# A decoder layer on one core: the cross-attention sums and gates in TensorE column groups, the normalisations on ScalarE, and another order on every engine

## The chip, the core and the metric

The kernel runs on one core of a Trainium2 chip. The metric is the device time of one execution in microseconds, the median of several runs.
Engines: PE is TensorE (PEld its weight loads), DVE is VectorE, ACT is ScalarE, POOL is GpSimd, SP is SyncE, which here only issues DMAs.

## The reference, cut to what matters

The input is 64 sequences of 128 tokens with 512 features; each goes through three steps, each followed by a residual and a layer normalisation.

```
x = layernorm(x + attn(x));  x = layernorm(x + xattn(x, ctx, ctx));  x = layernorm(x + ffn(x))

attn:   q, k, v = x @ W.T + b (rotary on q, k); per token, its 16 heads of 32 attend to each other; @ Wo.T + bo
xattn:  q = x, k = v = ctx, 16 heads of dh = 32, causal
        ig, fg   = concat(q, k, v) @ Wi + bi,  ... @ Wf + bf          # (token, head)
        log_D    = cumsum(log_sigmoid(fg)) differences + ig, masked to s >= t
        D        = exp(log_D - max_log_D);  C = (q k^T / sqrt(dh)) * D
        Cn       = C / (max(|C.sum(-1)|, exp(-max_log_D)) + 1e-6)
        h        = Cn @ v;  each head of h normalised over its 32 features, * ln_scale
ffn:    eight experts score each token; the best one applies a rank-8 update and a bias
```

## The kernel before

One sequence is one tile of 128 tokens by 512 features, and the tiles go through a software pipeline. In step a, each engine works on tile a and on older ones: b = a-1, c = a-2, d = a-3 and so on. The order of the pieces inside a step is written out by hand, once for each engine; a piece waits on semaphores of the pieces that it reads from. There are 64 tiles and 6 steps more to drain (`LAGS`).

The pieces, by their names in the code: `p_*` makes q, k, v of tile a or b; `a_S`, `a_O`, `a_proj` are the attention among heads; `m_*` is the cross-attention; `r_*` its head normalisation and residual; `x_*` the experts and the output.
q, k, v and the projection are `product` (L365 to L368; v is L355 to L360): twelve matmuls of 512 columns each. The other matmuls are float32, and each stands as two instructions in the trace.

What the change touches, tile by tile:

- `m_gate` (L460, L462): the gates of tile c, from x1T and cT, in eight matmuls with 48 stationary columns, summed in one place.
- `m_gs`, `m_abs`, `m_softplus`, `m_scan`: log-sigmoid, running sum `Fs`, `a_row`, running maximum `M_row` and `FM`, on 16 partitions, shared between ACT and DVE.
- `spread_M` (SP): `M_row` goes out to DRAM and comes back broadcast over the partitions into `Mb` (1 MB). `m_Dx` (ACT, L642) makes 16 exponentials of 128x128 from it, `m_mask` (POOL, L739) cuts them to the triangle, `m_QK` (PE, L481) makes the products of q and k in four row groups, and `m_C` (DVE, L913) multiplies the two into `Dx`.
- `m_c1` (PE, L448): the context times a centring matrix, so that every head has mean zero; ACT copies it to `c1`, which has a 33rd column of ones for each head.
- `heads` (PE, L493): 16 matmuls, each with a 128x128 block of `Dx` as the stationary operand and 33 columns of `c1` moving; ACT copies the result to `Hs` (`m_Hs`, L650).
- `r_norm`, `r_var`, `r_pow` (POOL, L746), `r_y` (DVE, L939), `r_y2` and `r_r2` (POOL): head normalisation and residual.
- three layer normalisations: statistics on DVE (`norm_stats`), `rsqrt` by a power on POOL (L760), and then `a_x1` (L884), `r_x2` (L952), `x_yo` (L1021), each a subtract and multiply over 512 columns, on DVE.

In PE's step the end of one step and the start of the next read:

```
m_QK(c)  m_x1T(b)  x_F(e)  x_LT(f) | m_gate(c)  a_S(b)  m_H(d)  heads(d, 0, 5)  p_v(b)  heads(d, 5, H)  p_v_rest(b)
m_cT(b)  m_aT(c)  m_c1(c)  p_VG(b)  x_Y(g)  p_xT(a)  a_O(b)  x_x2T(e)  p_q(a)  a_proj(b)  p_k(a)
```

Of the kernel before, what the change touches and what calls it, by code (L numbers as in the profile page):

```python
# [20 lines left out]
ALU = mybir.AluOpType  # L21
# [31 lines left out]
LAGS = 6  # L53
PADS = 7
# [48 lines left out]
def bass_decoder(nc, x, ctx, wq, wk, wv, wo, bqkv, bo, rope, ident, mask_l, mask_r, head_rows,  # L103
                 w_gate, b_gate, ln_scale, w_expert, debias, degen, expert_rows, out):
    with ExitStack() as stack:
# [3 lines left out]
        def sem(name):  # L109
# [10 lines left out]
        center = sb("center", [P, P])  # L120
# [13 lines left out]
        zeros = sb("zeros", [H, P])  # L134
# [20 lines left out]
        rs1 = sb("rs1", [P, 1])  # L155
        x1 = [sb(f"x1_{i}", [P, E]) for i in range(2)]

        cb = [sb(f"cb{i}", [P, E]) for i in range(2)]
        c1 = sb("c1", [P, H, HD])
        x1T = [sb(f"x1T{i}", [P, CH, P]) for i in range(2)]  # L160
        cT = [sb(f"cT{i}", [P, CH, P]) for i in range(2)]
        gs = sb("gs", [GW, P])
# [3 lines left out]
        log_f = sb("log_f", [H, P])  # L166
        Fs = sb("Fs", [H, P])
# [8 lines left out]

        Hs = sb("Hs", [P, H, HD])
# [12 lines left out]
        rs2 = sb("rs2", [P, 1])  # L190
        x2 = [sb(f"x2_{i}", [P, E]) for i in range(2)]
        rs2sq = sb("rs2sq", [P, 1])
# [25 lines left out]
        rs3 = sb("rs3", [P, 1])  # L218
        yo = sb("yo", [P, E])
# [5 lines left out]
            shift_set pads_set high_set low_set center_set""".split()  # L225
        each = """xT_ps xhigh_sb xlow_sb q_ps k_ps v_ps QT_sb KT_sb VT_sb VG_ps VG_sb xres_sb
            S_ps max_sb sub_sb ex_sb sum_sb rec_sb exn_sb PT_sb
            O_ps Ohigh_sb Olow_sb proj_ps r1_sb st1_sb mv1_sb ve1_sb rs1_sb x1_sb
            x1T_ps x1T_sb cT_ps cT_sb c1_ps c1_sb gate_ps gs_sb gabs_sb gexp_sb gln_sb logf_sb
            Fs_sb a_sb M_sb FM_sb aT_ps acol_sb QK_ps H_ps Hs_sb sq_sb  # L230
            hn0_sb hn1_sb hn2_sb hnn_sb hvar_sb hve_sb hrs_sb y1_sb y2_sb r2_sb
            st2_sb mv2_sb ve2_sb rs2_sb x2_sb rs2sq_sb
            x2T_ps x2T_sb F_ps fz_sb fz2_sb fn1_sb fn2_sb fn3_sb fs_sb fu_sb fv_sb fe_sb fe1_sb
            gate_sb gmax_sb gkey_sb gkmax_sb oh_sb L_sb LT_ps LT_sb Y_ps y3_sb st3_sb mv3_sb
            ve3_sb rs3_sb yo_sb""".split()
# [51 lines left out]
        def _(sp):  # L287
# [35 lines left out]
            def step(a):  # L323
                n2, n1, c, f = a.older(-2), a.older(-1), a.older(1), a.older(6)
                if n2.real():
                    sp.wait_ge(s.xT_ps, upto(n2, 2))
                    load_x(n2)
                if n1.real():
                    sp.wait_ge(s.cT_ps, upto(n1, 2))
                    load_ctx(n1)  # L330
# [11 lines left out]
        def _(pe):  # L342
# [10 lines left out]
            def high_part(b, high, n, lo, hi):  # L353
                for c in range(lo, hi):
                    mm(bank[b][:], high[:, c, :], w_high[n][:, c, :], start=False, stop=False)  # L355
                    mm(bank[b][:], high[:, c, :], w_low[n][:, c, :], start=False, stop=False)  # L356

            def low_part(b, low, n):
                for c in range(CH):
                    last = mm(bank[b][:], low[:, c, :], w_high[n][:, c, :], start=False, stop=c == CH - 1)  # L360
                return last

# [8 lines left out]
            def p_xT(t):  # L371
                pe.wait_ge(s.x_in[t.parity()], landed(t, 4))
                edge(pe, t, (s.cT_sb, 1), (s.r1_sb, 2), (s.x1T_sb, 2))
                transposes(bank[5], xb[t.parity()]).then_inc(s.xT_ps, 1)

            def p_q(t):
# [3 lines left out]
                edge(pe, t, (s.xhigh_sb, 0), (s.VT_sb, 1), (s.VG_sb, 1), (s.fn1_sb, 5))  # L380
# [3 lines left out]
            def p_k(t):  # L384
                pe.wait_ge(s.x2T_sb, upto(t, 4))
                edge(pe, t, (s.xhigh_sb, 0), (s.xlow_sb, 0), (s.Hs_sb, 3), (s.acol_sb, 2), (s.y3_sb, 6), (s.LT_sb, 6))
# [3 lines left out]
            def p_v(t):  # L390
                edge(pe, t, (s.xhigh_sb, 0), (s.xlow_sb, 0), (s.VG_sb, 1), (s.QT_sb, 0), (s.fn1_sb, 4))
                bias(4, 2)
                high_part(4, x_high, 2, 0, 2)

            def p_v_rest(t):
                high_part(4, x_high, 2, 2, CH)
                low_part(4, x_low, 2).then_inc(s.v_ps, 1)

            def p_VG(t):
                pe.wait_ge(s.VT_sb, upto(t))  # L400
                edge(pe, t, (s.QT_sb, 0), (s.fn1_sb, 4))
                transposes(bank[4], VT).then_inc(s.VG_ps, 1)

            def a_S(t):
                for j in range(4):
                    pe.wait_ge(s.C_sb[j], upto(t, 2))
                edge(pe, t, (s.QT_sb, 0), (s.KT_sb, 0), (s.Ohigh_sb, 1), (s.Olow_sb, 1))
# [11 lines left out]
            def a_O(t):  # L419
# [3 lines left out]
                edge(pe, t, (s.sub_sb, 0), *[(s.C_sb[j], 2) for j in range(4)])  # L423
# [9 lines left out]
            def a_proj(t):  # L433
                pe.wait_ge(s.Olow_sb, upto(t))
                edge(pe, t, (s.Ohigh_sb, 0), (s.cT_sb, 0), (s.xlow_sb, -1), (s.x1T_sb, 1))
# [4 lines left out]
            def m_cT(t):  # L440
                pe.wait_ge(s.c_in[t.parity()], landed(t, 1))
                edge(pe, t, (s.xlow_sb, 0), (s.r1_sb, 1), (s.x1T_sb, 1))
                transposes(bank[5], cb[t.parity()]).then_inc(s.cT_ps, 1)

            def m_c1(t):
                edge(pe, t, (s.cT_sb, 0), (s.gs_sb, 0), (s.Hs_sb, 1))
                for c in range(CH):
                    last = mm(bank[7][:, c * P:(c + 1) * P], cT[t.parity()][:, c, :], center[:], start=True, stop=True)  # L448
                last.then_inc(s.c1_ps, 1)

            def m_x1T(t):
                pe.wait_ge(s.x1_sb, upto(t))
                edge(pe, t, (s.cT_sb, 0), (s.xlow_sb, -1), (s.r1_sb, 0))
                transposes(bank[5], x1[t.parity()]).then_inc(s.x1T_ps, 1)

            def m_gate(t):
                pe.wait_ge(s.x1T_sb, upto(t))
                edge(pe, t, (s.cT_sb, 0), (s.c1_sb, 1), (s.Hs_sb, 2))
                for n in range(CH):
                    mm(bank[7][0:GW, 0:P], wg_sb[:, 0, n, :], x1T[t.parity()][:, n, :], start=(n == 0), stop=False)  # L460
                for n in range(CH):
                    last = mm(bank[7][0:GW, 0:P], wg_ctx[:, n, :], cT[t.parity()][:, n, :], start=False,  # L462
                              stop=(n == CH - 1))
                last.then_inc(s.gate_ps, 1)

            def m_aT(t):
# [3 lines left out]
                edge(pe, t, (s.y3_sb, 5), (s.x2T_sb, 3), (s.KT_sb, -1), (s.LT_sb, 4))  # L470
                nc.tensor.transpose(bank[6][:, 0:H], a_row[:], id_sb[0:H, 0:H])
                nc.tensor.transpose(bank[6][:, H:2 * H], FM[:], id_sb[0:H, 0:H]).then_inc(s.aT_ps, 1)

            def m_QK(t):
                for j in range(3):
                    pe.wait_ge(s.Dm_sb[j], upto(t))
                edge(pe, t, (s.x1T_sb, 0), (s.cT_sb, 0), (s.sub_sb, -1), (s.Ohigh_sb, -1), (s.Olow_sb, -1))
# [724 lines left out]
```

## Time and profile before

| what | value |
|---|---|
| three runs | 1919.57, 1921.3, 1925.41 us; median 1921.3 |
| profiled execution, first to last instruction | 1919.0 us |
| PE matmuls busy | 1766.6 us, 92% |
| DVE busy | 1557.8 us, 81% |
| ACT busy | 783.8 us, 41% |
| POOL busy | 759.3 us, 40% |
| DMA | 141.14 MB, 74 GB/s on the mean |

The profiled execution has no time of its own beside its span: the 1919.0 us are counted from its first to its last instruction, and lie 2.3 us under the median of the runs. Shares are of that span. A matmul's bar is longer than the slot that it takes, since matmuls are pipelined; the distance from one start to the next is what it costs.

### The profile page before, as it was taken

Reading aid. Unit: us, or ns where it says so; the run is one execution under the profiler, and the core shown is the slowest. Engines: PE = TensorE matmul, PEld = TensorE weight load, DVE = VectorE, ACT = ScalarE, POOL = GpSimd, SP = SyncE. Lnnn points to the kernel's source line nnn. Section 1 sums busy time; section 2 is a strip of 40 time slices with the busy share of each in tenths; the row PEclk is TensorE's granted clock in tenths of the full one; section 3 lists DMA queues with packets and bytes.
Section 4 is the critical chain, followed back from the end, with each engine's and each line's share of the span. In section 5 each row is a group of like instructions: output and inputs, shape, how many; then the busy total and the mean of one; then the engine's idle time right before and its main releaser. Section 6 shows DMA issues by size and latency. Waiting matters only on the chain.

```text
span 1919.0 us, 67339 instructions
## 1 busy us (share of the span) xinstructions
PE 1766.6 (92%) x27529; PEld 1464.6 (76%) x27656; DVE 1557.8 (81%) x3898; ACT 783.8 (41%) x2193; POOL 759.3 (40%) x779
## 2 busy tenths in 40 slices
PE   0889999999999999999999999999999999999985
PEld 0678787887887788788778778878877877887863
DVE  4456888888888888888888888888888888888876
ACT  2134344434434434443443444444344344444431
POOL 1034344334434433433443443343344344334333
PEclk9999999999999999999999999999999999999985
DMA  4112222221221222222122222222212222222110
GB/s 138 60 58 75 70 67 84 78 82 60 82 77 66 80 75 67 79 81 78 63 80 77 66 82 73 69 77 82 77 66 77 77 66 82 74 76 69 66 57 28
DMA packets 53829, 141.14 MB, mean 74 GB/s; under 512 B 8767, under 2 KB 10431, under 8 KB 45578
## 3 DMA queue, kind: packets, MB, share of 16 engines
q1 hardware_dynamic: 53770, 140.31, 21.4%
q8 instruction: 42, 0.69, 0.1%
q14 instruction: 17, 0.14, 0.0%
HBM read 122.98 MB, written 17.30 MB: 73 GB/s over the span
## 4 chain that ended last, share of the span: by engine, by line
PE 83%; DVE 6%; ACT 6%; issue 3%; SPq 1%; POOL 0%; DMA 0%; POOLq 0%; ACTq 0%; DVEq 0%
PE bank L493 12%; PE bank L365 10%; PE bank L366 9%; PE bank L368 9%; PE bank L347 8%; PE bank L355 4%; PE quad L481 4%; PE bank L448 4%; PE bank L460 3%; PE bank L507 3%; PE bank L360 3%; PE bank L356 3%; PE bank L519 3%; PE bank L462 3%; ACT x_high L584 2%
## 5 line engine op out<-in xcount | busy, mean ns | idle before, releaser
L734 POOL TENSOR_TENSOR ex<-ex,w_rec 128x512 f32<-128x512 f32 x64 | 67.2, 1050 | 766.4 <-DVE w_rec L848 766.4
L642 ACT ACTIVATE Dx<-Mb,a_col 128x128 f32<-128x128 f32 x1024 | 313.0, 397 | 0.0
L493 PEld LDWEIGHTS bank<-c,Dx 128*128 128x128 f32 x2048 | 244.4, 192 | 30.1 <-ACT LT L672 21.6
L493 PE MATMUL bank<-c,Dx 128*128 128x33 f32 x2048 | 246.7, 276 | 17.1 <-ACT LT L672 14.7
L746 POOL TENSOR_TENSOR h_rs<-h_ve,half_neg 128x16 f32<-128x16 f32 x64 | 186.9, 2921 | 147.1 <-DVE h_ve L934 147.1
L615 ACT ACTIVATE x1T<-bank 128x512 f32<-128x512 f32 x64 | 38.3, 598 | 357.8 <-PE bank L347 357.8
L913 DVE SCALAR_TENSOR_TENSOR Dx<-quad,Dx 128x512 f32<-128x512 f32 x256 | 159.0, 683 | 11.5 <-PE quad L481 2.8
L760 POOL TENSOR_TENSOR rs<-ve,half_neg 128x1 f32<-128x1 f32 x192 | 106.1, 553 | 155.0 <-DVE ve L869 154.9
L739 POOL TENSOR_SCALAR_AFFINE_SELECT Dx<-Dx 128x512 f32<-128x512 f32 x256 | 159.8, 637 | 5.4 <-ACT Dx L642 5.4
L594 ACT ACTIVATE ex<-ex 128x512 f32<-128x512 f32 x64 | 40.3, 630 | 239.3 <-DVE ex L839 239.3
L347 PE MATMUL bank<-id_sb,x 128*128 128x128 f32 x512 | 85.7, 291 | 54.9 <-DVE x2sq L954 53.0
L355 PE MATMUL bank<-wv_high,x_high 128*128 128x512 f32 x256 | 118.5, 463 | 0.0
L365 PE MATMUL bank<-wq_high,x_high 128*128 128x512 f32 x256 | 116.9, 457 | 0.0
L365 PE MATMUL bank<-wk_high,x_high 128*128 128x512 f32 x256 | 113.1, 442 | 0.0
L347 PEld LDWEIGHTS bank<-id_sb,x 128*128 128x128 f32 x512 | 54.8, 142 | 74.4 <-DVE x2sq L954 64.4
L366 PE MATMUL bank<-wq_low,x_high 128*128 128x512 f32 x256 | 103.7, 405 | 0.0
L365 PE MATMUL bank<-wo_high,O_high 128*128 128x512 f32 x256 | 101.5, 396 | 1.0 <-DVE O_low L858 1.0
L750 POOL TENSOR_TENSOR r<-r,lns_sb 128x512 f32<-128x512 f32 x64 | 83.3, 1301 | 47.8 <-DVE r L939 47.8
L356 PE MATMUL bank<-wv_low,x_high 128*128 128x512 f32 x256 | 101.1, 395 | 0.0
L366 PE MATMUL bank<-wo_low,O_high 128*128 128x512 f32 x256 | 101.1, 395 | 0.0
L366 PE MATMUL bank<-wk_low,x_high 128*128 128x512 f32 x256 | 101.0, 395 | 0.0
L864 DVE BATCH_NORM_STATS2 st<-r 128x6 f32<-128x512 f32 x128 | 88.9, 694 | 4.1
(157 smaller groups left out, 4351.5 us busy)
## 6 DMA issues: line engine op xcount, KB each, us to landing
Mb<-m_rows SPq DMA_DIRECT2D x64, 1024.0 KB, 4.6
xb<-in_x SPq DMA_DIRECT2D x256, 64.0 KB
xr<-in_x SPq DMA_DIRECT2D x64, 256.0 KB, 2.6
cb<-in_ctx SPq DMA_DIRECT2D x64, 256.0 KB, 3.5
out_dram<-yo SPq DMA_DIRECT2D x64, 256.0 KB, 2.4
Dx<-in_wq SPq DMA_DIRECT2D x4, 256.0 KB, 4.5
Dx<-in_wk SPq DMA_DIRECT2D x4, 256.0 KB, 5.5
Mb<-in_wv SPq DMA_DIRECT2D x4, 256.0 KB, 5.6
```

The source lines that it names most:

```text
L347: last = nc.tensor.transpose(dst[:, c * P:(c + 1) * P], src[:, c * P:(c + 1) * P], id_sb[:])
L355: mm(bank[b][:], high[:, c, :], w_high[n][:, c, :], start=False, stop=False)
L356: mm(bank[b][:], high[:, c, :], w_low[n][:, c, :], start=False, stop=False)
L365: mm(bank[b][:], high[:, c, :], w_high[n][:, c, :], start=first and c == 0, stop=False)
L366: mm(bank[b][:], high[:, c, :], w_low[n][:, c, :], start=False, stop=False)
L368: last = mm(bank[b][:], low[:, c, :], w_high[n][:, c, :], start=False, stop=c == CH - 1)
L493: last = mm(bank[6 + h // 8][:, (h % 8) * HD:(h % 8 + 1) * HD], Dx[t.parity()][:, h % 4, h // 4, :], c1[:, h, :], start=True, stop=True)
L642: last = go(Dx[t.parity()][:, j, n, :], Mb[t.parity()][:, h, :], ACT.Exp, bias=a_col[t.parity()][:, h:h + 1], scale=-1.0)
L739: nc.gpsimd.affine_select(Dx[t.parity()][:, j], Dx[t.parity()][:, j], compare_op=ALU.is_ge, fill=0.0, base=0, pattern=[[0, CH], [1, P]], c ...
L746: tt(h_rs[:], h_ve[:], half_neg[:], ALU.pow).then_inc(s.hrs_sb, 1)
L760: tt(rs[:], ve[:], half_neg[:, 0:1], ALU.pow).then_inc(rs_sem, 1)
L913: stt(out=Dx[t.parity()][:, j], in0=quad[:, j, :].rearrange("p (c n) -> p c n", n=P), scalar=float(D) ** -0.5, in1=Dx[t.parity()][:, j], o ...
```

## The change

It does the following.

- The sums over keys are turned round. `m_HT` has `c1` (32 columns for each head) as the stationary operand and a 128x128 block of `Dx` moving, in four column groups of 32 (`tile_position=(0, 32 * j)`); ACT copies the result to `HT`, and `m_H` multiplies each of its four blocks with `back`, which turns it back and centres it. `m_c1` on PE and its copy on ACT are gone; a new `m_c1` on POOL takes the first feature of every head from the others, which leaves a column of ones free.
- The gates come as four partial sums in four column groups (`m_part`), are copied by ACT (`m_g4`), and are added by one matmul with `pick` (`m_gate`).
- `m_softplus` makes the log-sigmoid from the gates on ACT alone; DVE scans it (`m_scan`).
- `a_x1`, `r_x2` and `x_yo` become ACT activations with a scale and a bias; POOL makes these in `rsqrt` from mean and variance (an addition, the power, a product). `r_y` moves to POOL ahead of the two operations there.
- Every engine's order is new, with one step more to drain (`LAGS` 7), and many semaphore waits that others already cover are gone.

The diff, cut to its core:

```diff
+            def m_part(t):
+                pe.wait_ge(s.x1T_sb, upto(t))
+                edge(pe, t, (s.cT_sb, 0))
+                for n in range(CH):
+                    mm(bank[5][32 * n:32 * n + 32, 0:P], wg_x1[:, n, :], x1T[t.parity()][:, n, :], start=True, stop=False,
+                       tile_position=(0, 32 * n))
+                for n in range(CH):
+                    last = mm(bank[5][32 * n:32 * n + 32, 0:P], wg_ctx[:, n, :], cT[t.parity()][:, n, :], start=False,
+                              stop=True, tile_position=(0, 32 * n))
             def m_gate(t):
+                pe.wait_ge(s.g4_sb, upto(t))
+                mm(bank[5][0:GW, P:2 * P], pick[:], g4[:], start=True, stop=True).then_inc(s.gate_ps, 1)
+            def m_HT(t):
+                pe.wait_ge(s.LT_sb, upto(t, 3))
+                pe.wait_ge(s.c1_sb, upto(t))
+                for n in range(CH):
+                    for j in range(4):
+                        last = mm(bank[7][32 * j:32 * j + 32, n * P:(n + 1) * P], c1[t.parity()][:, 4 * n + j, :],
+                                  Dx[t.parity()][:, j, n, :], start=True, stop=True, tile_position=(0, 32 * j))
             def m_H(t):
+                pe.wait_ge(s.HT_sb, upto(t))
+                for n in range(CH):
+                    last = mm(bank[6 + n // 2][:, (n % 2) * 4 * HD:(n % 2 + 1) * 4 * HD], HT[:, n * P:(n + 1) * P],
+                              back[:].rearrange("p h d -> p (h d)"), start=True, stop=True)
...
+PE     a_S(b) m_part(c) m_HT(d) m_gate(c) p_v(b) m_cT(b) m_H(d) p_VG(b) p_xT(a) m_aT(c) x_Y(g) a_O(b)
+       p_q(a) x_x2T(e) a_proj(b) m_QK(c) p_k(a) x_F(e) x_LT(f) m_x1T(b)
+ACT    m_x1T(c) x_LT(g) x_yo(h) m_g4(c) a_exp(b) m_HT(d) m_softplus(c) x_exp(f) m_cT(b) m_Hs(d) p_VG(b)
+       p_xT(a) r_sq(d) m_acol(c) a_O(b) r_x2(e) m_Dx(c, 2) x_x2T(e) m_Dx(c, 0) m_Dx(c, 1) m_Dx(c, 3) a_x1(b)
+POOL   rsqrt(e) x_square(e) p_xres(a) a_scale(b) m_c1(b) r_pow(d) r_y(d) m_mask(c, 2, 0, 1, 3) rsqrt(b) rsqrt(g)
+DVE    r_stats(e) x_shift(f) a_max(b) a_sub(b) x_choose(f) a_sum(b) a_rec(b) m_scan(c) p_VT(b) a_PT(b)
+       r_norm(d) p_low(a) r_var(d) x_y3(g) a_low(b) x_stats(g) x_gate(f) p_QT(a) a_r1(b) a_stats(b)
+       m_C(c, 2, 0, 1, 3) p_KT(a)
...
+            def a_x1(t):                                                       # ACT
+                act.wait_ge(s.nm1_sb, upto(t))
+                go(x1[t.parity()][:], r1[:], ACT.Identity, bias=nm1[:], scale=rs1[:]).then_inc(s.x1_sb, 1)
+            def m_c1(t):                                                       # POOL
+                tt(c1[t.parity()][:, :, 1:D], heads[:, :, 1:D], heads[:, :, 0:1].broadcast_to([P, H, D - 1]),
+                   ALU.subtract).then_inc(s.c1_sb, 1)
+            def r_y(t):                                                        # POOL
+                tt(r2[:].rearrange("p (h d) -> p h d", d=D), Hs[:, :, 0:D],
+                   h_rs[:].unsqueeze(2).broadcast_to([P, H, D]), ALU.mult).then_inc(s.y1_sb, 1)
                 tt(r2[:], r2[:], lns_sb[:], ALU.mult).then_inc(s.y2_sb, 1)
                 tt(r2[:], r2[:], x1[t.parity()][:], ALU.add).then_inc(s.r2_sb, 1)
+            def rsqrt(t, mv, ve, rs, nm, mv_sem, ve_sem, rs_sem, nm_sem, used): # POOL
+                tt(ve[:], mv[:, 1:2], eps[:], ALU.add).then_inc(ve_sem, 1)
                 tt(rs[:], ve[:], half_neg[:, 0:1], ALU.pow).then_inc(rs_sem, 1)
+                ts(nm[:], mv[:, 0:1], rs[:], -1.0, ALU.mult, ALU.mult).then_inc(nm_sem, 1)
             def m_scan(t):                                                     # DVE
                 dve.wait_ge(s.gln_sb, upto(t))
+                nc.vector.tensor_tensor_scan(Gs[:], g_relu[32:GW, :], g_ln[32:GW, :], 0.0, ALU.add, ALU.add)
+                tt(a_row[:], gs[:], Gs[:], ALU.add).then_inc(s.a_sb, 1)
                 nc.vector.tensor_tensor_scan(M_row[:], a_row[:], a_row[:], -3.0e38, ALU.max, ALU.max)
+                tt(FM[:], M_row[:], Gs[:], ALU.subtract).then_inc(s.FM_sb, 1)
```

The four orders are written in one line each here; in the code they are calls. The constants `back`, `pick`, `wg_x1` and `wg_ctx` are made once, ahead of the first tile.

## Rows read from the trace of the kernel before

**Rows 1.** The chain of work that ended last, shares of the span by engine.
```profile
PE 83%; DVE 6%; ACT 6%; issue 3%; SPq 1%; POOL 0%; DMA 0%; POOLq 0%; ACTq 0%; DVEq 0%
```

**Rows 2.** Step's window: us; busy us (instructions) of PE, PEld, DVE, ACT, POOL; clock, DMA.
```profile
985.00:1013.19 28.19, 27.14 (x432) 22.62 (x434) 24.11 (x61) 12.09 (x34) 11.75 (x12) 1.00 0.22 75
```

**Rows 3.** Timeline of PE, the matmuls that open `a_S`: tiles 0, 3, 63.
```profile
62.94 0.38 PE L409 MATMUL quad<-pair_r,pair_l 33*128 33x128 bf16 x4 [1.11 <-DVE KT L808]
...
137.57 0.40 PE L409 MATMUL quad<-pair_r,pair_l 33*128 33x128 bf16 x4
...
1832.36 0.39 PE L409 MATMUL quad<-pair_r,pair_l 33*128 33x128 bf16 x4
```

**Rows 4.** Timeline of PE in one step: start, us, instruction, [idle before it].
```profile
1000.86 0.66 PE L347 MATMUL bank<-id_sb,x 128*128 128x128 f32 x4 [0.84 <-DVE x2sq L954]
...
1010.31 1.17 PE L481 MATMUL quad<-x1T,cT 32*128 32x128 f32 x32
1011.41 0.66 PE L347 MATMUL bank<-id_sb,x 128*128 128x128 f32 x4
...
1013.03 1.07 PE L460 MATMUL bank<-x1T,wg_sb 128*48 128x128 f32 x8
...
1014.92 0.39 PE L409 MATMUL quad<-pair_r,pair_l 33*128 33x128 bf16 x4
...
1016.73 1.30 PE L493 MATMUL bank<-c,Dx 128*128 128x33 f32 x10 [0.21 <-ACT LT L672]
1017.90 0.58 PE L355 MATMUL bank<-wv_high,x_high 128*128 128x512 f32 x1
...
1019.02 2.54 PE L493 MATMUL bank<-c,Dx 128*128 128x33 f32 x22
1021.39 0.48 PE L355 MATMUL bank<-wv_high,x_high 128*128 128x512 f32 x1
...
1024.10 1.16 PE L448 MATMUL bank<-center,cT 128*128 128x128 f32 x8
1025.10 0.60 PE L347 MATMUL bank<-id_sb,VT 128*128 128x128 f32 x4
```

**Rows 5.** Timeline of DVE: set-up, `a_rec` of tile 0, one operation of `x_gate`.
```profile
25.47 1.43 DVE L1044 TENSOR_SCALAR Dx<-Dx 128x512 f32<-128x512 f32 x4 [15.59 <-DMA Mb<-in_wo]
...
67.41 0.25 DVE L848 RECIPROCAL w_rec<-w_sum 128x16 f32<-128x16 f32 x1
...
1005.19 1.28 DVE L1002 TENSOR_TENSOR L<-fz,L 128x64 f32<-128x64 f32 x1
```

**Rows 6.** Timeline of POOL: `p_xres`, and `r_pow`, in the same steps.
```profile
1005.08 1.31 POOL L730 TENSOR_TENSOR xr<-xr,bo_sb 128x512 f32<-128x512 f32 x1
...
1026.02 2.91 POOL L746 TENSOR_TENSOR h_rs<-h_ve,half_neg 128x16 f32<-128x16 f32 x1 [2.23 <-DVE h_ve L934]
```

**Rows 7.** Groups of POOL by line, 400 to 1500 us: busy us, mean ns, idle.
```profile
L739 POOL TENSOR_SCALAR_AFFINE_SELECT Dx<-Dx 128x512 f32<-128x512 f32 x156 | 97.4, 636 | 0.0
L760 POOL TENSOR_TENSOR rs<-ve,half_neg 128x1 f32<-128x1 f32 x117 | 64.1, 548 | 70.5 <-DVE ve L869 70.5
...
L734 POOL TENSOR_TENSOR ex<-ex,w_rec 128x512 f32<-128x512 f32 x39 | 41.0, 1051 | 461.5 <-DVE w_rec L848 461.5
```

**Rows 8.** Groups of DVE by line, 400 to 1500 us.
```profile
L939 DVE TENSOR_TENSOR r<-Hs,h_rs 128x512 f32<-128x512 f32 x39 | 26.8, 688 | 0.0
...
L905 DVE TENSOR_TENSOR_SCAN M_row<-a_row 16x128 f32<-16x128 f32 x39 | 16.1, 412 | 3.0
```

**Rows 9.** Timeline of ACT: twelve of `m_Dx`'s exponentials, and `m_Hs`.
```profile
1001.27 3.61 ACT L642 ACTIVATE Dx<-Mb,a_col 128x128 f32<-128x128 f32 x12
...
1021.60 0.67 ACT L650 ACTIVATE Hs<-bank 128x264 f32<-128x264 f32 x2 [0.79 <-PE bank L493]
```

**Rows 10.** DMA issues by tensor: count, KB each, us to landing.
```profile
Mb<-m_rows SPq DMA_DIRECT2D x64, 1024.0 KB, 4.6
...
m_rows<-M_row SPq DMA_DIRECT2D x64, 8.0 KB, 1.3
```

More of the change, by code:

```diff
@@ L45 @@
 ML_EPS = 1e-6
-LAGS = 6
-PADS = 7
+LAGS = 7
+PADS = 15
+MATS = 25
 PEEL = 10
@@ L528, in _ @@
             pe.wait_ge(s.bias_step, 15)
-            pe.wait_ge(s.center_set, 11)
+            pe.wait_ge(s.mats_set, MATS)
             def step(a):
                 b, c, d, e, f, g = [a.older(n) for n in range(1, 7)]
+                if b.real():
+                    a_S(b)
+                if c.real():
+                    m_part(c)
+                if d.real():
+                    m_HT(d)
                 if c.real():
@@ L685, in step @@
             def step(a):
-                b, c, d, e, f = [a.older(n) for n in range(1, 6)]
+                b, c, d, e, f, g, h = [a.older(n) for n in range(1, 8)]
+                if c.real():
+                    m_x1T(c)
+                if g.real():
+                    x_LT(g)
+                if h.real():
+                    x_yo(h)
+                if c.real():
+                    m_g4(c)
+                if b.real():
+                    a_exp(b)
                 if d.real():
-                    r_sq(d)
+                    m_HT(d)
+                if c.real():
+                    m_softplus(c)
                 if f.real():
@@ L708, in step @@
                 if c.real():
+                    m_Dx(c, 0)
+                    m_Dx(c, 1)
                     m_Dx(c, 3)
                 if b.real():
-                    m_x1T(b)
-                    m_gs(b)
-                    m_softplus(b)
-                if f.real():
-                    x_LT(f)
-                if a.real():
-                    a_exp(a)
-                if c.real():
-                    m_Hs(c)
+                    a_x1(b)
             steps(act, step)
@@ L766, in _ @@
+            for c in range(CH):
+                tt(wg_ctx[:, c].rearrange("p (a n) -> p a n", n=H), part[:, 1, c], part[:, 2, c],
+                   ALU.add).then_inc(s.pads_set, 1)
+                nc.gpsimd.tensor_copy(wg_x1[:, c].rearrange("p (a n) -> p a n", n=H), part[:, 0, c]).then_inc(s.pads_set, 1)
+            ts(bg_neg[:], bg_sb[:], -1.0, 1.0, ALU.mult, ALU.mult).then_inc(s.pads_set, 1)
             pool.wait_ge(s.pads_set, PADS)
@@ new lines, in _ @@
+            dve.wait_ge(s.mats_set, 16)
+            nc.vector.tensor_copy(pick[:].rearrange("p (a n) -> p a n", n=H)[:, 0:3:2, :],
+                                  pick2[:].rearrange("p (a n) -> p a n", n=H)).then_inc(s.mats_set, 1)
+            for i in range(4):
+                nc.vector.memset(back[32 * i:32 * i + 1, :, :], 0.0).then_inc(s.mats_set, 1)
+            dve.wait_ge(s.mats_set, 21)
+            for i in range(4):
+                nc.vector.memset(back[32 * i:32 * i + 1, i, D:HD], 1.0).then_inc(s.mats_set, 1)
```

415 lines of the change are left out of this document (183 added, 232 removed).

## The prediction

> **What bounds the kernel now.** I read the chain that ended last first: 83% of it lies on PE, 6% each on DVE and ACT [rows 1]. An average can hide stages with other limits, so the next view is the busy time in a window one step long: PE 27.14 of 28.19 us, DVE 24.11, ACT 12.09, POOL 11.75, at full clock throughout [rows 2]. The step repeats: the matmuls that open `a_S` stand at 137.57 us for tile 3 and at 1832.36 us for tile 63, so 60 steps took 1694.79 us, 28.25 each [rows 3]. What lies around them (137.57 ahead, 1919.0 - 1832.36 = 86.6 behind) is filling and draining. Inside one step PE's timeline shows two visible waits, 0.84 us ahead of the transposes of x2 and 0.21 ahead of `heads` [rows 4], together the 1.05 us that PE is not busy. So the kernel is bound by PE's work, instruction after instruction, and only then by waits. DVE stands at 86% of the step and would be the next bound.
>
> **The change on PE.** Slots are read from start to start [rows 4]. Removed from each step: the gates, 1013.03 to 1014.92, 1.89 us; `heads`, 1016.73 to 1017.90 and 1019.02 to 1021.39, 1.17 + 2.37 = 3.54; the centring, 1024.10 to 1025.10, 1.00. Together 6.43.
>
> Added: `m_HT` (16 matmuls, 32 instructions, 128 moving columns), `m_part` (16 instructions), `pick` (2), and `m_H` (8 instructions of 132 columns). The last two are of the centring's form, eight in 1.00 us: 0.25 + 1.00. For the first two no row has column groups. The nearest rows bound them. From below, `m_QK`: 32 instructions of 128 columns in four row groups, 1010.31 to 1011.41, 34 ns each, as the groups work at the same time. From above, the gates as they are: sixteen in 1.89 us, 118 ns each, one after the other. That makes `m_HT` 1.10 to 3.78 and `m_part` 0.55 to 1.89. I take the lower ends: the shapes are those of `m_QK` with rows and columns exchanged, and the four groups write different partitions. Added: 1.10 + 0.55 + 0.25 + 1.00 = 2.90. PE's work for one step becomes 27.14 - 6.43 + 2.90 = 23.61 us (27.63 at the upper ends).
>
> The Trainium skill, "TensorE: Matmul & The Clock Gate", Part 3, gives 2.38 times for three column tiles and 3.07 times for four row tiles; by an estimate from it four column tiles would give about 3.1 times, and the two pieces (3.78 + 1.89) / 3.1 = 1.83 us in place of 1.65. No run here shows a column group yet.
>
> **The waits that the new order brings.** I count from the opening matmul of `a_S` and add up the slots in the new order.
>
> *`p_VG` behind `m_scan`.* PE: `a_S` 1.60 (1014.92 to 1016.73, less the wait), `m_part` 0.55, `m_HT` 1.10, `pick` 0.25, v and `m_cT` 3.6 (1017.90 to 1019.02, and 1021.39 to 1024.10 without 0.2 for `m_aT`), `m_H` 1.0: at 8.1 PE asks for VT [rows 4]. DVE: tile 0's `a_rec` ended 67.66 - 62.94 = 4.72 us after its scores' opening [rows 3, 5]; `x_choose`, eight small operations, now fills the wait for the exponential there; I give it 0.4 beyond that wait, so 5.1. Then `m_scan` stands in front of `p_VT`. Its four operations read two operands from SBUF, and so does POOL's work at that time. What that costs stands in one pair of rows: DVE's multiplication started at 1005.19 took 1.28 us and ended 0.08 after POOL's addition of 1005.08 ended [rows 5, 6]. In 5.1 to 7.2 POOL runs `a_scale` (1.05 us [rows 7]) and directly after it the new `m_c1`, a form not in the trace: 1.05 as `a_scale`, which broadcasts too, to 1.31 as `p_xres`; I take 1.05. So the second operation of `m_scan` ends at about 7.25, the running maximum (0.41 [rows 8]) and the last addition bring it to 8.0, `p_VT` to 8.7: PE waits 0.6, and 0.7 with the handover. Without the collision DVE would be at `p_VT` by 7 and the wait nothing; with a longer `m_c1` it is 0.95. I take 0.7.
>
> *POOL's chain to x1.* `m_H` ends at 8.1, `m_Hs` starts at 8.3. In before, `r_pow` started 4.42 us after `m_Hs` (1021.60 to 1026.02 [rows 6, 9]); the new order puts two copies of ACT and `p_low` between, and takes DVE's transposes out, so I keep 4: 12.3. `r_pow` 2.9; `r_y` three operations, 1.05 + 1.31 + 1.31 [rows 6, 7] (on DVE the first took 0.69 [rows 8]); four masks of 0.64; `rsqrt` 0.55 and two small operations, not in the trace, between nothing and a power's 0.55 each, 0.25 taken [rows 7]; x1 on ACT 0.65, as `m_Hs`'s two copies [rows 9]. 12.3 + 2.9 + 3.7 + 2.5 + 1.1 + 0.65 = 23.2. PE comes to `m_x1T`, last in its step, at 23.61 + 0.7 - 0.5 = 23.8 (0.5: four transposes, at half of the centring's eight). So this is hidden with 0.6 to spare, and would be the first to show.
>
> The Trainium skill, "GPSIMD Engine Reference", section 4.1, speaks against such a move: two-input element work is about twice as slow on GpSimd as on VectorE. By it `r_y`'s first operation would take 1.4 us and not 1.05, and the spare time shrink to 0.25. The trace has 1.05 and 1.31 on POOL against 0.69 for DVE.
>
> *The row maximum's way.* `M_row` is ready at 7.7. `spread_M` is SP's last piece of the step before, so SP has nothing queued in front; 1.3 + 4.6 us later [rows 10] `Mb` has landed, at about 13.8. Sixteen exponentials at 0.30 [rows 9] and one copy of x2T between: 19.1. POOL reaches its last mask later (21.4), so this costs nothing, with some 2 us to spare. The 1 MB of `Mb` now runs beside the loads of x, four DMAs that SP issues after it; a delay of 2 us would be needed.
>
> **What costs nothing.** The three normalisations and `m_gs` put about 3 us on ACT, 15 of 24; it loses the copy of the centred context and gains that of `HT`. DVE loses `r_y`, three normalisations and small operations, some 4 us, so 20 of 24: neither bounds. Without that relief DVE's 24.11 [rows 2] would have been the next bound. `x_yo` needs the store of the tile before; SP issues it after r1, most of a step earlier. Set-up's new small operations come before the weights land at 25.47, where DVE sat idle 15.59 us [rows 5].
>
> **Sum.** A step is 23.61 + 0.7 = 24.3 us against 28.25: 3.95 saved, and 60 of them 237 us. Filling gains about 1 us a step, draining loses as much on POOL's longer chain and the seventh step; I set both at nothing. 1919.0 - 237 = 1682; with the 2.3 us by which the median stands above the span, 1684.
>
> **The rivals.**
> - *POOL's chain decides*: if `r_pow` starts a full 4.4 us behind `m_Hs` and the small operations cost a power each, with POOL's operations held up by DVE as DVE is by them, the chain is 1 to 2 us longer and the step 24.7 to 26.2: 1708 to 1798, 1742 in the middle. For it speaks that everything on POOL from `r_pow` to x1 is now serial; against it the 0.6 us to spare.
> - *Column groups overlap by half*: all four read the same 128 partitions at once, where `m_QK`'s read 32 each. At 59 ns the two pieces take 2.8 us, the step 25.5: 1756.
> - *They do not overlap*, and the change does not do what it says: 118 ns, work 27.63; `m_scan` then has time, so hardly a wait: 1884.
> - *Slower than before*: column groups one after the other, and their weight loads not hidden either. The break-even is a price for each of the 48 instructions: the rest of PE's work is 21.96 us, so (28.25 - 21.96) / 48 = 131 ns. At 150 ns the step is 29.2 and the time 1978. Against it: in `heads` a weight load of the full width for every 33 columns fits in 3.54 / 32 = 111 ns [rows 4].
>
> The Trainium skill, "TensorEngine Tiling (Array Packing)", Tiling Modes, says that a change of tiling mode drains TensorE. By it the new neighbours (32x32, 128x32, full width) would cost a few drains a step. The trace has `m_QK`, between two full-width pieces, at 1.10 us with both changes in it, so the sum holds them.
>
> **How the numbers follow.** My forecast, a step of 24.0 to 24.7 us, 0.53, its own range 1664 to 1708. POOL's chain 0.18; half overlap 0.10; no overlap 0.08; slower 0.09; better than 1655 (no wait at all: 23.6 a step gives 1643) 0.02. From 1650 to 1800 lie the first three, 0.81. A change of 0.3% (6 us) is about what a measurement tells from none. No overlap is faster in three of four such cases and within 0.3% in the rest: faster 0.89, same 0.02, slower 0.09.
>
> **What would show it.** In the profile after: `m_HT` 1.1 us from its first instruction to `pick`; `m_part` 0.55; PE's two old waits gone and one of about 0.7 us ahead of VT's transposes, released by DVE, with `a_row`'s addition on DVE ending together with `m_c1` on POOL; `a_x1` released by POOL with PE hardly waiting behind it; a distance of 24.3 us between the openings of `a_S`. It is wrong if PE waits a microsecond or more ahead of x1's transposes, or if 32 instructions of `m_HT` fill more than 1.7 us.

## The result, and the profile after

The changed kernel takes 2037.2 us (median of 4 runs, 2030.1 to 2044.7) against 1923.4 us for the kernel before on the same chip: 1.059 times as long, 95% interval 1.056 to 1.063. The prediction was 1684 us, 1650 to 1800, so it missed on the wrong side. The profiled execution has a span of 2042.9 us.

The chain that ended last in the kernel after, by engine, stands against [rows 1]; from its queue table comes the row of the instruction queue (packets, MB, share), and from the table of 40 slices the clock.

```profile
PEclk9999999998898988888988889888989888998885
...
q8 instruction: 276, 4.52, 0.9%
...
PE 72%; issue 15%; DVE 8%; ACT 3%; SPq 1%; DMA 1%; POOL 0%; DVEq 0%; POOLq 0%; ACTq 0%
```

"issue", time in which PE waits for nothing that the profile shows, rose from 3% to 15%. That queue brings program code, by its name, and the runs below bear it out. Its row in the kernel before, of which the prediction says nothing, has 42 packets:

```profile
q8 instruction: 42, 0.69, 0.1%
```

The 4.52 MB in 276 packets are 16 KB each. In the trace of before no packet of this queue lies between 352.0 and 1830.5 us of the span; in that of after they come nine to a round of the loop (a round is two steps). The loop has 27 rounds; the first loads its code in both kernels, and the other 26 load it again in after: 42 + 26 x 9 = 276.

Timeline of PE, openings of `a_S` in after (the four matmuls that begin a step), the counterpart of [rows 3]: tiles 3 and 63.

```profile
135.79 0.38 PE L406 MATMUL quad<-pair_r,pair_l 33*128 33x128 bf16 x4 [0.64 <-DVE KT L852]
...
1956.52 0.39 PE L406 MATMUL quad<-pair_r,pair_l 33*128 33x128 bf16 x4
```

So a step takes (1956.52 - 135.79) / 60 = 30.35 us, not the forecast 24.3 and not 28.25 as before. What PE waits for from 400 to 1500 us (us in all, times, longest):

```profile
PE quad L412 <- issue: 56.6, 35, 2.2
PE quad L425 <- issue: 56.3, 18, 4.1
PE quad L406 <- issue: 55.9, 18, 3.4
PE bank L357 <- DVE VT L852: 8.9, 9, 1.1
```

The forecast wait for VT is there, with 8.9 us in all; 168.8 us are waits that no engine releases. PE's timeline over one round, cut to the places where they stand:

```profile
933.26 0.39 PE L406 MATMUL quad<-pair_r,pair_l 33*128 33x128 bf16 x4
933.59 1.24 PE L412 MATMUL quad<-KT,QT 32*32 32x32 f32 x122
936.12 0.26 PE L412 MATMUL quad<-KT,QT 32*32 32x32 f32 x6 [1.29 <-issue]
...
936.80 1.95 PE L485 MATMUL bank<-Dx,c 128*32 128x128 f32 x32
...
962.68 0.38 PE L406 MATMUL quad<-pair_r,pair_l 33*128 33x128 bf16 x4 [2.88 <-issue]
963.00 0.65 PE L412 MATMUL quad<-KT,QT 32*32 32x32 f32 x53
965.40 1.03 PE L412 MATMUL quad<-KT,QT 32*32 32x32 f32 x75 [1.75 <-issue]
...
981.30 0.67 PE L425 MATMUL quad<-PT,VG 32*32 32x32 f32 x39 [3.56 <-issue]
...
995.05 0.40 PE L406 MATMUL quad<-pair_r,pair_l 33*128 33x128 bf16 x4
995.37 1.24 PE L412 MATMUL quad<-KT,QT 32*32 32x32 f32 x122
997.91 0.26 PE L412 MATMUL quad<-KT,QT 32*32 32x32 f32 x6 [1.30 <-issue]
```

The waits stand at fixed instructions: at the head of the loop, after 53 of the first step's 128 scores (the 32x32 products of q and k in `a_S`), after 89 of its 128 small products of O, after 122 of the second step's scores, and again at the same place one round later (997.91). A wait for another engine would stand in front of a whole stage; these break a run of equal matmuls. `m_HT` at 936.80 takes 1.95 us against 1.06 where nothing was late ahead of it (below). The granted clock of those 1.95 us, the last column but two, is 0.50, its lower level of 1.2 GHz:

```profile
936.80:938.75 1.95, 1.95 (x41) 1.56 (x31) 1.85 (x8) 0.91 (x2) 0.00 (x0) 0.50 0.04 8
```

That gives a theory. TensorE's program is loaded in blocks of 16 KB. The compiled programs show 1758 TensorE instructions in a round before and 1768 after (a round in a window below has 869 matmuls and 869 weight loads; the rest are waits, registers and the branch). They show 149 fewer ahead of the loop in after, mainly waits that the change dropped from the steps written out ahead of it (`edge` only waits there). At two instructions a score, the 53rd score of the first step and the 122nd of the second lie 1768 / 2 + 2 x 69 = 1022 instructions apart, four times 256 within two. If the first step's break is the end of a block, the loop of after begins about 130 instructions into a block, and that of before, with 149 more ahead of it, about 23: 23 + 1758 = 1781 ends inside a seventh block (7 x 256 = 1792), 130 + 1768 = 1898 in an eighth. The Trainium skill, "Advanced Engine Details and Errata", ISA Cache, gives lines of 16 KB or 256 instructions, which agrees with the packets and the places of the waits, and 128 KB for TensorE, which would be eight such lines. The runs below put the limit for this loop at seven.

### The profile page after: what moved, and what is told of

The parts are those of the page before. It is cut to its first block, busy times and chain, and to the rows that moved or that the text cites. A ratio compares the mean times of both kernels' runs of the same rounds, so it can differ in the third digit from the quotient of the medians.

```text
span 2042.9 us, 67738 instructions
## 1 busy us (share of the span) xinstructions
PE 1667.0 (82%) x27595; PEld 1321.6 (65%) x27784; DVE 1321.7 (65%) x3206; ACT 973.2 (48%) x2577; POOL 1004.4 (49%) x1365
## 3 DMA queue, kind: packets, MB, share of 16 engines
q8 instruction: 276, 4.52, 0.9%
## 4 chain that ended last, share of the span: by engine, by line
PE 72%; issue 15%; DVE 8%; ACT 3%; SPq 1%; DMA 1%; POOL 0%; DVEq 0%; POOLq 0%; ACTq 0%
PE bank L365 15%; PE bank L366 11%; PE bank L368 10%; PE bank L357 7%; PE quad L425 5%; PE quad L412 5%; PE bank L485 4%; PE bank L518 3%; PE quad L475 3%; PE bank L507 3%; PE bank L493 2%; PE quad L406 1%; PE bank L452 1%; PE bank L461 1%; DVE a_row L929 1%
## 5 line engine op out<-in xcount | busy, mean ns | idle before, releaser
L878 DVE TENSOR_REDUCE neg_max<-quad 128x16 f32<-128x512 f32 x64 | 44.3, 691 | 263.1 <-PE quad L412 263.1
L425 PEld LDWEIGHTS quad<-PT,VG 32*32 32x32 f32 x8192 | 86.6, 106 | 144.2 <-issue 142.3
L425 PE MATMUL quad<-PT,VG 32*32 32x32 f32 x8192 | 99.6, 205 | 93.5 <-issue 92.8
L412 PE MATMUL quad<-KT,QT 32*32 32x32 f32 x8192 | 99.6, 214 | 85.3 <-issue 85.3
L412 PEld LDWEIGHTS quad<-KT,QT 32*32 32x32 f32 x8192 | 84.9, 112 | 99.3 <-issue 92.4
L365 PE MATMUL bank<-wq_high,x_high 128*128 128x512 f32 x256 | 141.2, 551 | 3.4 <-issue 3.3
L902 DVE TENSOR_TENSOR O_low<-quad,O_high 128x512 fp32r<-128x512 f32 x64 | 45.0, 704 | 133.8 <-ACT O_high L594 133.8
L594 ACT ACTIVATE O_high<-quad 128x512 fp32r<-128x512 f32 x64 | 42.3, 662 | 183.3 <-PE quad L425 183.3
L600 ACT ACTIVATE x<-r,nm,rs 128x512 f32<-128x512 f32 x64 | 52.2, 815 | 159.2 <-POOL nm L798 159.2
L485 PE MATMUL bank<-Dx,c 128*32 128x128 f32 x2048 | 103.9, 366 | 3.9 <-DVE Dx L941 2.8
```

The source lines that it names most:

```text
L365: mm(bank[b][:], high[:, c, :], w_high[n][:, c, :], start=first and c == 0, stop=False)
L412: last = mm(quad[32 * c:32 * c + 32, w, 32 * v:32 * v + 32], QT[rows, cols], KT[rows, cols], start=False, stop=True, skip_group_check=True ...
L425: last = mm(quad[32 * w:32 * w + 32, c, 32 * v:32 * v + 32], VG[rows, v, 32 * w:32 * w + 32], PT[rows, w, v, :], start=True, stop=True, sk ...
L485: last = mm(bank[7][32 * j:32 * j + 32, n * P:(n + 1) * P], c1[t.parity()][:, 4 * n + j, :], Dx[t.parity()][:, j, n, :], start=True, stop= ...
```

## The experiments

**Theory 1**: the loop, moved by the change, lies across one block more than TensorE keeps, and is loaded anew in each round. **Theory 2**: TensorE's new neighbours (column groups beside small products and full-width ones) cost the time. `a138`, `a60` and `a170` are the kernel after with so many instructions more ahead of TensorE's loop, `b107` is the kernel before with 107. The instructions are waits that are already met, two to an instruction.

```diff
 pe.wait_ge(s.const_in, CONST_IN)
+for _ in range(276):            # a138; 120 in a60, 340 in a170, 214 in b107
+    pe.wait_ge(s.const_in, CONST_IN)
```

> The changed kernel with 138 more instructions on TensorE's queue ahead of its loop, waits on a semaphore that has long arrived; the loop itself is as it is. Theory 1 (code loading): the loop's body, about 1,770 instructions, lies over eight blocks of 256 instructions (16 KB) and is fetched anew in every round; 138 instructions more push its start to the head of a block, so that it lies over seven, as I count it for the kernel before. Then the instruction queue moves nothing between the loop's first round and its end, the issue waits in the scores and the mixing are gone, the clock stays at 1.0, a step takes 24 to 25 us, the whole 1680 to 1730. Theory 2 (the waits come from the new neighbours on TensorE, column groups next to 32x32 groups, and the fetches are an accompaniment): nothing changes, 2025 to 2045 us.

> The same with 60 more instructions: by my count the loop still lies over eight blocks, only elsewhere in them. Theory 1: still fetched every round, about nine fetches of 16 KB per two steps, 2000 to 2060 us, with the issue waits at other instructions (60 instructions earlier in the body). Theory 2: 2025 to 2045 us, waits at the same instructions as in the changed kernel.

> The same with 170 more instructions, which by my count puts the loop's last 15 to 25 instructions into an eighth block. Theory 1 in its strict form (seven blocks or all is fetched anew): about 2000 to 2060 us. In a soft form (one or two blocks fetched per round): 1720 to 1800. Theory 2: 2025 to 2045 us.

> The kernel before with 107 more instructions ahead of TensorE's loop, so that its body lies in the blocks as that of the changed kernel does, over eight of them. Theory 1: it is now fetched in every round, some 230 more fetches, issue waits appear on TensorE, the clock falls below 0.95, and the time goes to 2150 to 2300 us. Theory 2: 1915 to 1930 us, no change.

| kernel | loop starts at | ends at | packets | time, us |
|---|---|---|---|---|
| after | 130 | 1898 | 276 | 2037.2 (4 runs) |
| `a60` | 190 | 1958 | 276 | 2051.2 (one run) |
| `a138` | 12 | 1780 | 42 | 1719.0 (1718.3 to 1719.6, 4 runs) |
| `a170` | 44 | 1812 | 123 | 1812.6 (one run) |
| before | 23 | 1781 | 42 | 1921.2 (7 runs) |
| `b107` | 130 | 1888 | 277 | 2080.1 (one run) |

"starts" and "ends" count instructions from the head of the block in which the loop begins, by the counts above. With 138 instructions more, and nothing else changed, the kernel takes 0.894 times the time of before, interval 0.892 to 0.897. The row of its queue, as in before:

```profile
q8 instruction: 42, 0.69, 0.2%
```

The kernel before, with 107 more, gets slower by 8%, though less than the 2150 to 2300 us expected. Theory 2 falls: the neighbours are the same in all four kernels with the change. `a60` confirms the place as well: there the scores of the loop's first step break after 23 instead of 53, 30 scores or 60 instructions earlier, as expected. PE's timeline:

```profile
983.41 0.31 PE L412 MATMUL quad<-KT,QT 32*32 32x32 f32 x23
986.12 1.34 PE L412 MATMUL quad<-KT,QT 32*32 32x32 f32 x105 [2.40 <-issue]
```

`a170`, with its loop twenty instructions into an eighth block, loaded in only 9 of its 26 rounds, and its time lies between the two ranges that were expected; why it was spared in the others stays open.

One round of after and one of `a138` show how the loss divides. Busy time in a window of after, then of `a138` (columns as in [rows 2]):

```profile
933.26:995.05 61.79, 52.31 (x864) 41.64 (x869) 40.57 (x98) 30.01 (x80) 31.06 (x42) 0.89 0.21 71
```

```profile
992.89:1042.17 49.28, 47.00 (x869) 37.82 (x869) 39.97 (x98) 30.02 (x80) 31.26 (x42) 1.00 0.25 85
```

PE idle is 9.48 us against 2.28: 7.20 more of waiting, net of 2.28 for VT that vanish in after. PE busy is 5.31 us longer at the same work: stretches at 1.2 GHz behind the waits, mean clock 0.89 against 1.00. Together that is 12.51 us a round, and 26 rounds of it make 325. The spans of the two profiled executions, 2042.9 and 1717.9 us, differ by 325.0, the medians by 318.

`a394` moves the loop by one whole block more; `a138_in40` leaves its start alone and adds 20 such instructions to each step inside it; `a_short` takes half of the scores out of after, with nothing added.

```diff
+for _ in range(788):            # a394: in place of 276, ahead of the loop
+    pe.wait_ge(s.const_in, CONST_IN)
 ...
+if a.regs is not None:          # a138_in40: in PE's step, in the loop alone
+    for _ in range(40):
+        pe.wait_ge(s.const_in, CONST_IN)
 ...
-for v in range(4):              # a_short: in a_S
+for v in range(2):
```

> The kernel after with 394 more instructions ahead of TensorE's loop, 138 and 256 more (all waits that are met already). Theory 1 (what decides is the place of the loop's start in a block of 256 instructions): the same as with 138, no fetches in the loop, 1719 us within 6 (one block more, 43 packets). Rival (what decides is the number of instructions that stand ahead, or the room that is left behind them): another time, 1750 to 2050 us.

> The kernel after with 138 more instructions ahead of TensorE's loop (1719.0 us), and 20 more in each step of the loop alone (waits that are met already), so that a round has 40 more: 1809 instead of 1768. Theory 1: from its start near the head of a block the loop now ends some 30 instructions into an eighth block, so fetches come back inside the loop: 100 to 276 packets and 1800 to 2050 us. Rival (twenty instructions cost only their own time): no fetches in the loop, 42 packets, and 1719 to 1780 us.

> The kernel after without any added instructions, but with half of the scores left out (keys of two of four groups: 64 of 128 small products per step), so that TensorE's loop has some 1512 instructions instead of 1768. This leaves out part of the computation. Theory 1 (a loop that does not lie within seven blocks of 256 instructions is loaded anew in each round): a loop of 1512 lies within seven blocks at any place, so there are no fetches in the loop, about 42 packets on the instruction queue, and the time is some 1660 to 1700 us (1719 less 64 steps of 0.65 us of scores). Rival: what is loaded depends on the place of the loop alone (its start in a block), which has hardly moved: some 270 packets, and about 1950 to 2020 us.

`a394`: 1726.7 us, one run, 43 packets, as theory 1 says, though 2 us above the 1725 that it allowed. In the loop its steps are as in `a138`, 24.63 us; what it has more lies ahead of the loop. It is the place within a block that decides, not how much stands ahead. `a138_in40`: 1947.0 us, 276 packets. Some forty instructions that wait for nothing cost 228 us, 9 us a round. Its queue row, and PE's longest kind of wait there, 400 to 1500 us:

```profile
q8 instruction: 276, 4.52, 1.0%
```

```profile
PE quad L406 <- issue: 120.8, 38, 5.7
```

`a_short`: 36 packets, none of them in the loop after its first round, so theory 1 held for the packets, with the loop of 1512 instructions too short to reach an eighth block. The time, 1768.0 us, missed the range of 1660 to 1700, for a reason of its own. With fewer scores PE comes to VT's transposes earlier and waits longer, 1.65 us instead of 1.13, so the time saved in the scores goes into the wait; and in part of the steps q's product behind that wait runs at the lower clock. Two steps of `a_short`: PE's timeline, then their windows.

```profile
558.79 0.66 PE L357 MATMUL bank<-id_sb,VT 128*128 128x128 f32 x4 [1.64 <-DVE VT L852]
...
1024.42 0.66 PE L357 MATMUL bank<-id_sb,VT 128*128 128x128 f32 x4 [1.65 <-DVE VT L852]
...
1030.18 0.63 PE L365 MATMUL bank<-wq_high,x_high 128*128 128x512 f32 x1
```

```profile
549.85:574.46 24.61, 22.97 (x368) 18.37 (x371) 21.23 (x49) 15.10 (x40) 15.61 (x21) 1.00 0.25 86
...
1015.47:1042.69 27.22, 25.57 (x369) 19.98 (x371) 22.20 (x49) 14.97 (x40) 15.67 (x21) 0.87 0.22 77
```

The first step takes 24.61 us at full clock, no less than `a138`'s 24.64 with all its scores. The second takes 27.22 at a mean clock of 0.87, with matmuls of q at 0.63 us, where the first has 0.39. Of the 51 steps from tile 12 to tile 63, 18 are near 27.2 us, 24 near 24.6 and nine between. The wait is the same in both steps shown, so its length alone does not decide whether the clock falls; what does stays open.

**What the change is worth without the loading.** PE's timeline of one step of `a138`:

```profile
1017.53 0.39 PE L406 MATMUL quad<-pair_r,pair_l 33*128 33x128 bf16 x4
1017.86 1.29 PE L412 MATMUL quad<-KT,QT 32*32 32x32 f32 x128
1019.07 0.42 PE L452 MATMUL bank<-x1T,wg_x 128*32 128x128 f32 x8
...
1019.53 1.06 PE L485 MATMUL bank<-Dx,c 128*32 128x128 f32 x32
1020.52 0.42 PE L461 MATMUL bank<-g,pick 128*48 128x128 f32 x2
1020.87 0.39 PE L361 MATMUL bank<-bias,ones_bf 128*128 128x512 bf16 x1
...
1024.29 1.07 PE L493 MATMUL bank<-back,HT 128*128 128x132 f32 x8
1026.49 0.66 PE L357 MATMUL bank<-id_sb,VT 128*128 128x128 f32 x4 [1.13 <-DVE VT L854]
```

From start to start: `m_part` 0.46 us, `m_HT` 0.99, `pick` 0.35, and `m_H` 1026.49 - 1.13 - 1024.29 = 1.07. The counterparts in [rows 4] took 1.89, 3.54 and 1.00. `a138_onegroup` puts `m_HT` into a single column group, which leaves three quarters of its outputs unwritten:

```diff
-last = mm(bank[7][32 * j:32 * j + 32, ...], ..., tile_position=(0, 32 * j))
+last = mm(bank[7][0:32, ...], ..., tile_position=(0, 0))
```

> The kernel after with 138 more instructions ahead of TensorE's loop (1719.0 us), with all 32 products of the sums over keys (m_HT) in one column group, so that three quarters of their outputs are not written. Theory (products in four column groups run beside one another, which is why 32 of them take 0.99 us): in one group the 32 take 3.2 to 3.8 us, the step grows by 2.2 to 2.8 us and the time comes to 1860 to 1900 us. Rival (the 32 products are short whatever their group is, because only 32 columns are loaded): HT stays near 1.0 us and the time near 1719 us.

It took 1796.9 us, one run. PE's timeline there:

```profile
1007.46 3.66 PE L485 MATMUL bank<-Dx,c 128*32 128x128 f32 x32
1011.05 0.42 PE L461 MATMUL bank<-g,pick 128*48 128x128 f32 x2
```

`m_HT` takes 3.59 us instead of 0.99: the four groups run beside one another, 31 ns for an instruction against 112. (The edit also makes four products write to one place. That this is not what costs is argued, not tested: `heads` in [rows 4], which did not, took 3.54 / 32 = 111 ns an instruction.) The size of `m_HT` was as expected, the time was not (1860 to 1900), because PE now comes later to VT and the wait of 1.13 is gone. That leaves 2.60 - 1.13 = 1.47, and the step grew by 1.31, from 24.64 to 25.95.

The wait for VT itself: DVE's timeline in the same step of `a138`, then POOL's.

```profile
1023.35 0.66 DVE L928 TENSOR_TENSOR_SCAN Gs<-g_relu,g_ln 16x128 f32<-16x128 f32 x1 [0.75 <-ACT g_ln L633]
1024.04 0.92 DVE L931 TENSOR_TENSOR a_row<-gs,Gs 16x128 f32<-16x128 f32 x1
...
1025.53 0.28 DVE L938 TENSOR_TENSOR FM<-M_row,Gs 16x128 f32<-16x128 f32 x1
1025.74 0.70 DVE L854 STREAM_TRANSPOSE VT<-bank 128x512 f32<-128x512 f32 x1
```

```profile
1022.68 1.05 POOL L761 TENSOR_TENSOR ex<-ex,w_rec 128x512 f32<-128x512 f32 x1 [2.04 <-DVE w_rec L894]
1023.69 1.13 POOL L767 TENSOR_TENSOR c<-cb 128x496 f32<-128x496 f32 x1
```

Two things are late ahead of VT. DVE stands idle for 0.75 us ahead of `m_scan`, for ACT's logarithm `g_ln`. And the addition of `m_scan` into `a_row` takes 0.92 us and ends at 1024.96, with `m_c1` on POOL ending at 1024.82, where the same form takes 0.28 at 1025.53. `a138_c1first` puts `m_c1` ahead of `a_scale` on POOL; `a138_vtfirst` puts `p_VT` ahead of `m_scan` on DVE; `a138_both` does both.

```diff
 if b.real():                 # POOL, a138_c1first
-    a_scale(b)
     m_c1(b)
+    a_scale(b)
 ...
+if b.real():                 # DVE, a138_vtfirst
+    p_VT(b)
     ... m_scan(c) ...
-    p_VT(b)
     a_PT(b)
```

> The kernel after with 138 more instructions ahead of TensorE's loop (1719.0 us), and on GpSimd the subtraction of ctx's first columns (m_c1) now ahead of the scaling of the probabilities (a_scale). What is to be told apart: why TensorE still waits 1.13 to 1.15 us in each step ahead of the transposes of V*gate. Theory A (GpSimd and VectorE slow one another: m_scan's two-input operation on VectorE runs while m_c1 runs on GpSimd, so p_VT behind it is late): with m_c1 done earlier, the wait falls from 1.14 to some 0.2 us, the step from 24.66 to some 23.7 us and the time to some 1660 us. Theory B (the wait comes from something else ahead of VT on VectorE or from its inputs): the wait stays at 1.1 us and the time within 5 us of 1719. Rival C: a_scale now comes 1.2 us later, so the transpose of the probabilities (a_PT) and with it O is late, and the time rises to some 1740 to 1790 us.

> The kernel after with 138 more instructions ahead of TensorE's loop (1719.0 us), and on VectorE the transpose of V (p_VT) now ahead of m_scan instead of behind it. Theory A (V's transpose is late only because m_scan stands ahead of it): the wait of 1.14 us per step goes, the step comes to some 23.6 us and the time to 1655 to 1665 us; m_scan and with it the spread of M come some 1 us later, which is hidden. Theory B (V's transpose would have to wait for TensorE's own product anyway): the wait moves to VectorE and stays on the path, 1719 us within 5. Rival C: M comes late, the exponentials of Dx start later, and the heads (L485) wait: over 1730 us.

> The kernel after with 138 more instructions ahead of TensorE's loop, with both new orders: V's transpose ahead of m_scan on VectorE (alone 1675.7 us) and ctx's subtraction ahead of the scaling of the probabilities on GpSimd (alone 1707.1 us). If both take from the same wait ahead of the transposes of V*gate (0.01 us per step of it is left with V's transpose first), the second has nothing left to take there and puts the probabilities 1.2 us later: within 8 us of 1675.7 or above it. If they take from different waits, the gains add: some 1664 us.

`a138_c1first`: 1707.1 us (1701.2 to 1707.6), 0.887 of before, interval 0.884 to 0.890; some 12 us of the 59 that its theory A gave, and the wait for VT is still 43.7 us in 45 steps. The collision was real but only moved, as DVE's timeline there shows:

```profile
1014.62 1.16 DVE L928 TENSOR_TENSOR_SCAN Gs<-g_relu,g_ln 16x128 f32<-16x128 f32 x1 [0.25 <-ACT g_ln L633]
1015.81 0.28 DVE L931 TENSOR_TENSOR a_row<-gs,Gs 16x128 f32<-16x128 f32 x1
```

The addition is back at 0.28 us; the scan ahead of it, 0.66 in `a138`, is now the one that runs beside POOL (`a_scale`, 1014.45 to 1015.50) and takes 1.16.

`a138_vtfirst`: 1675.7 us (1671.6 to 1678.2), 0.871 of before, interval 0.868 to 0.874, some 11 us above the range of its theory A. The wait for VT is gone. `m_scan` now comes after POOL's `m_c1`, which ended at 1025.60, so DVE's timeline there shows what its two operations take undisturbed:

```profile
1025.70 0.41 DVE L928 TENSOR_TENSOR_SCAN Gs<-g_relu,g_ln 16x128 f32<-16x128 f32 x1
1026.15 0.28 DVE L931 TENSOR_TENSOR a_row<-gs,Gs 16x128 f32<-16x128 f32 x1
```

Together 0.69 us, against 1.58 in `a138` and 1.44 in `a138_c1first`, which is why the latter gained so little. PE's largest wait from 400 to 1500 us is a new one, for `FM`, `m_scan`'s last result, ahead of `m_aT`:

```profile
PE bank L467 <- DVE FM L938: 14.3, 46, 0.4
```

That is 0.31 us a step; the openings in its loop stand 23.77 us apart. `a138_both`: 1673.7 us (1672.9 to 1673.9), 0.870 of before, interval 0.868 to 0.872, no better than `a138_vtfirst` within what its runs differ by: both take from the same wait, as the first of the two expectations said. These two are the fastest found.

## Why the prediction was wrong

**The step that failed** is a term that the sum put at nothing without a reason: the loading of TensorE's program. "I set both at nothing" spoke of filling and draining, "What costs nothing" of other engines and the set-up, and nowhere is there a term for where TensorE's loop comes to lie in its program. The change took 149 instructions from the part ahead of the loop and added ten to a round, so that the loop reached into an eighth block. That term is 318 us, larger than the whole gain. None of the rivals had it. The slower rival had another mechanism, column groups one after the other with their weight loads in the open: its break-even was 131 ns for an instruction, and the trace of `a138` shows 31 in `m_HT`. So after came out slower by another way than that rival's. The sign that the prediction gave against itself, `m_HT` over 1.7 us, did show in after (1.95 at 936.80), but from the clock of 0.50 there.

**PE's work** was right. Added pieces 0.46 + 0.99 + 0.35 + 1.07 = 2.87 us, forecast 2.90; a step of `a138` without its wait 24.64 - 1.13 = 23.51, forecast 23.61. The choice of the lower ends, by `m_QK`'s row, holds, and `a138_onegroup` shows why.

**The wait for VT** was foreseen with its place, its releaser and the collision, but mis-sized: 1.13 us, not 0.7, so outside the stated 0 to 0.95. PE asked 7.83 us after the opening (forecast 8.1), and the transpose ended at 8.91 (forecast 8.7), so the size was missed by 0.27 us on PE's side and 0.2 on DVE's. The addition ended at 7.43 (7.25), right behind `m_c1` at 7.29 (7.2). That DVE came so close is in part luck: `m_scan` began at 5.82 and not 5.1, for the logarithm from ACT, last in its chain, was not in the working at all. "Without the collision" the wait was to be nothing. `m_scan`'s two operations lost 1.58 - 0.69 = 0.89 us beside POOL, so by an estimate from these rows 0.24 of the 1.13 would be left. No run tests it, since `a138_c1first` only moved the collision.

**POOL's chain to x1** was hidden, as forecast: in `a138`, with the opening at 1017.53, x1 was ready 23.65 us after it (forecast 23.2), and PE came to its transposes at 24.11 (23.8), without a wait. ACT's and PE's rows:

```profile
1040.37 0.81 ACT L602 ACTIVATE x<-r,nm,rs 128x512 f32<-128x512 f32 x1 [2.41 <-POOL nm L800]
1041.64 0.60 PE L357 MATMUL bank<-id_sb,x 128*128 128x128 f32 x4
```

That it "would be the first to show" was wrong: with VT's wait gone, `FM` showed first. **The row maximum's way** was hidden as well; `Mb` landed in 4.6 us, as before [rows 10].

**The sum**, even without loading in the loop, is 35 us too low: 1719 against 1684. PE's openings of `a_S` in `a138`, tiles 3, 12 and 63:

```profile
136.87 0.39 PE L406 MATMUL quad<-pair_r,pair_l 33*128 33x128 bf16 x4
...
376.70 0.39 PE L406 MATMUL quad<-pair_r,pair_l 33*128 33x128 bf16 x4
...
1634.31 0.40 PE L406 MATMUL quad<-pair_r,pair_l 33*128 33x128 bf16 x4
```

The last 51 of the 60 steps took 24.66 us instead of 24.3, 18 us in all. The first nine (six written out ahead of the loop, and the loop's first three, in which its code is loaded) took 26.65, another 21 us above the forecast. Filling and draining, set at no change, were 4 us shorter. Blocks arrive throughout the nine steps, 28 of the 42 packets between 137 and 340 us, and PE has 14 us of "issue" waits there. In the kernel before the same nine steps cost 28.58 against 28.19 in its loop, with 4 us of such waits: denser steps seem to feel the loading more, but no run tests that.

## What to carry to other kernels

Read the row of the instruction queue and the share of "issue" before and after any edit that changes the number of TensorE's instructions, including waits dropped far from the loop: where a loop nearly fills what the engine keeps of its program, a few dozen instructions decide over more time than the edit itself. A wait that breaks a run of equal matmuls at the same instruction in each round, with no engine releasing it, was code being loaded here; to test for it, shift the loop by waits that are already met. And a change that is slower as a whole may hold its gain intact: here 10.6% came back with 138 idle instructions, and 13% with one transpose moved.

## What the hardware showed that was not expected

- A TensorE loop that ended 1780 or 1781 instructions from the head of its first block was loaded once and then ran 26 rounds without a packet (`a138`, before); one that ended at 1821 (`a138_in40`) or beyond was loaded anew in each, nine packets a round. At 1812 (`a170`) it was loaded in 9 of 26 rounds. The Trainium skill, "Runtime: NRT & Kernel Launch", Instruction fetch mechanics, calls the cost of crossing a 16 KB boundary mostly hidden. Of nine blocks a round in after only four show as a wait, at the loop's head and in the runs of 32x32 products, but those four come to 9.48 us. What sets the limit at seven blocks rather than eight was not tried, nor why a loop that lies across eight loads nine.
- The waits cost again through the clock: 5.31 us more of busy time a round in after, with stretches at 1.2 GHz, beside 9.48 of waiting.
- Instructions on 128x32 weights in four column groups start 31 ns apart, 112 ns apart in one.
- A small operation of two SBUF operands on DVE took 0.92 us instead of 0.28 beside a two-operand one on POOL, and a scan 1.16 instead of 0.41.
